# Choosing 64 tokens of 512 in eight rounds of eight largest, and a scatter with two transfers in flight in place of eight

## The reference

```python
x = x + _L0_xattn_ref(_layernorm(x), ctx, ...)   # map attention
x = x + _L0_ffn_ref(_layernorm(x), ...)          # token choice, below
x = x + _L1_xattn_ref(_layernorm(x), ctx, ...)   # attention to the context
x = x + _L1_ffn_ref(_layernorm(x), ...)          # 32 routed experts, 6 per token, and 2 shared ones
```

```python
k = max(1, int(T * CAPACITY))                         # 64 of 512 tokens in each batch
scores = jnp.einsum('btd,d->bt', hidden_states, w_router)
_, idx = jax.lax.top_k(scores, k)
idx = jnp.sort(idx, axis=-1)
sel = hidden_states[b, idx]                           # 256 rows go through attention and an MLP
...
gated = gate * processed + (1.0 - gate) * x           # gate = sigmoid of the row's score
output = hidden_states.at[b, idx].set(gated.reshape(B, k, D))
```

## Time and profile before

| | us |
|---|---|
| median of 3 runs | 2518.43 (2517.94 to 2521.67) |
| the profiled execution, its own time | 2518.06 |
| its span, first to last instruction | 2516.1 |
| token choice, first normalized tile to first gather product | 153.56 to 210.57 |
| scatters, first to last issue | 1275.93 to 1399.72 |
| TensorE busy in the whole span | 1986.4 (79%) |
| VectorE busy | 1068.8 (42%) |
| GpSimd busy | 1147.9 (46%) |
| ScalarE busy | 530.5 (21%) |

### The profile page before, as it was taken

The page is one execution under the profiler, slowest core; times in us unless marked ns, Lnnn a source line. Parts: engine busy times, 40 slices in busy tenths (PEclk is TensorE's granted clock), DMA queues, the critical chain, the costliest instruction groups (busy, mean ns, idle before and its releaser), DMA issues.

```text
span 2516.1 us, 33335 instructions
## 1 busy us (share of the span) xinstructions
PE 1986.4 (79%) x10460; PEld 1427.2 (57%) x10461; DVE 1068.8 (42%) x2094; ACT 530.5 (21%) x1132; POOL 1147.9 (46%) x578
## 2 busy tenths in 40 slices
PE   6925887968845789986762599999999999999910
PEld 3413443433312333333751599999999999999910
DVE  2573442057664667753840243333333333333300
ACT  3300221101102455441110121121122112112200
POOL 0000000003552655553357204776855878781886
PEclk8966997989975899999885799999999999999965
DMA  3052003221124444542135112555544545552999
GB/s 106 0 152 80 15 27 116 93 76 51 67 83 129 152 147 159 165 151 60 46 141 207 60 44 73 179 156 161 181 157 149 176 153 188 172 183 76 204 159 192
DMA packets 200086, 307.42 MB, mean 122 GB/s; under 512 B 16673, under 2 KB 95153, under 8 KB 199761
## 3 DMA queue, kind: packets, MB, share of 16 engines
q1 hardware_dynamic: 129744, 180.77, 22.6%
q0 software_dynamic: 21504, 50.74, 8.9%
q10 hardware_dynamic: 48768, 74.98, 8.9%
HBM read 188.33 MB, written 118.10 MB: 122 GB/s over the span
## 4 chain that ended last, share of the span: by engine, by line
PE 40%; issue 5%; POOL 5%; DMA 1%; DVE 1%; ACT 0%; SPq 0%; POOLq 0%; DVEq 0%; ACTq 0%
PE psum L2122 15%; PE psum L2142 8%; PE psum L2127 8%; POOL X L1748 5%; PE psum L2147 4%; PE psum L2109 3%; PE psum L2116 2%; DMA X<-d_y,f_slots 1%; DVE r_score L1915 1%; PE psum L2080 0%; PE psum L2072 0%; DMA r_w_gate<-in_L_ffn_gate_w 0%; DVE r_score L1916 0%; DVE e_gu_low L1886 0%; ACT r_hot L1767 0%
## 5 line engine op out<-in xcount | busy, mean ns | idle before, releaser
L2122 PE MATMUL psum<-e_gu_high,e_rowT_high 128*128 (+1 forms) x1272 | 430.1, 340 | 10.3 <-issue 10.2
L2122 PE MATMUL psum<-e_gu_low,e_rowT_high 128*128 (+1 forms) x1272 | 412.1, 326 | 4.0 <-issue 4.0
L1775 ACT ACTIVATE e_silu<-psum 128x352 f32<-128x352 f32 x159 | 74.0, 466 | 961.0 <-PE psum L2127 850.4
L2127 PE MATMUL psum<-e_gu_high,e_rowT_low 128*128 (+1 forms) x1272 | 258.7, 325 | 22.2 <-DVE e_rowT_low L1843 12.8
L2122 PEld LDWEIGHTS psum<-e_gu_high,e_rowT_high 128*128 128x128 f32 x1272 | 241.4, 190 | 31.5 <-issue 26.8
L2122 PEld LDWEIGHTS psum<-e_gu_low,e_rowT_high 128*128 128x128 f32 x1272 | 242.5, 191 | 8.6 <-issue 4.3
L1685 POOL TENSOR_TENSOR e_gu_high<-e_gu_in,e_ones 128x1408 fp32r<-128x1408 f32 x33 | 83.7, 2536 | 323.4 <-PE psum L2127 315.9
L2127 PEld LDWEIGHTS psum<-e_gu_high,e_rowT_low 128*128 128x128 f32 x1272 | 215.3, 190 | 23.2 <-DVE e_rowT_low L1843 13.1
L2142 PE MATMUL psum<-e_d_high,e_midT_high 128*128 (+3 forms) x477 | 190.4, 399 | 46.5 <-issue 45.6
L1852 DVE TENSOR_TENSOR e_midT_low<-psum,e_midT_high 128x256 fp32r<-128x256 f32 x159 | 67.5, 425 | 350.8 <-ACT e_midT_high L1784 323.0
L2142 PE MATMUL psum<-e_d_low,e_midT_high 128*128 (+3 forms) x477 | 189.4, 397 | 0.0
(11 more groups left out here) (338 smaller groups left out, 3693.6 us busy)
## 6 DMA issues: line engine op xcount, KB each, us to landing
d_sorted<-y_zeros SPq DMA_DIRECT2D x32, 1040.0 KB, 8.6
d_y<-e_y ACTq DMA_DIRECT2D x127, 256.0 KB
e_row<-d_sorted ACTq DMA_DIRECT2D x125, 260.0 KB
e_gu_in<-in_L_ffn_w_gate SPq DMA_DIRECT2D x32, 704.0 KB, 4.4
e_gu_in<-in_L_ffn_w_up SPq DMA_DIRECT2D x32, 704.0 KB, 5.1
e_d_in<-in_L_ffn_w_down SPq DMA_DIRECT2D x32, 512.0 KB, 4.4
d_y<-y_zeros SPq DMA_DIRECT2D x8, 1024.0 KB, 5.5
e_d_in<-in_L_ffn_w_down SPq DMA_DIRECT2D x32, 192.0 KB, 4.9
```

The costliest lines, as they stand in the source:

```text
L2122: nc.tensor.matmul(bank[:, 0:M].unsqueeze(1), rowT_high[par][:, k, :], w[:, bass.ds(buffer, 1), k, at:at + M], start=(k == 0 and n == 0), ...
L2127: last = nc.tensor.matmul(bank[:, 0:M].unsqueeze(1), rowT_low[par][:, k, :], gu_high[:, bass.ds(buffer, 1), k, at:at + M], start=False, st ...
```

## The change

Token choice: ScalarE writes the normalized tiles as scale times X plus `shift`, VectorE only reduces them. The scores are transposed to one row of 512 for each batch on four partitions. Eight rounds of the eight largest (`max`) and their replacement by -3e38 (`match_replace`) mark 64 tokens; a running sum over the marks gives their slots, which are transposed back. The round trip of the scores through DRAM is gone. The residual adds come behind the one-hot tiles. SP issues the heads' weights, behind the small loads and with no wait. Scatter: `SCATTERS` is 2. The diff, with its removed lines cut where the section above tells them:

```diff
             @block.sync
+                for dst, src in ((slot_base[:], c.dram["i_slot_base"]), (iota[:], c.dram["i_count"]),
...
-                sp.wait_ge(score_T_ready, 1)
-                sp.dma_start(c.dram["d_scores"], score_T[:]).then_inc(score_stored, 16)
-                sp.wait_ge(score_stored, 16)
...
+                for k in range(CC):
+                    rows = slice(k * P, (k + 1) * P)
+                    for src, at, cols in ((c.dram["L0_ffn_wq"], 0, QH * DH), (c.dram["L0_ffn_wk"], QH * DH, DH),
+                                          (c.dram["L0_ffn_wv"], (QH + 1) * DH, DH)):
+                        sp.dma_start(w_heads[:, k, :, at:at + cols],
+                                     src[rows, :].rearrange("p (h n) -> p h n", n=cols)).then_inc(heads_loaded, 16)
             @block.vector
                 norm_rows_into(nc, dve, chain, c, mv, rstd, var_ready, rstd_ready, 1e-5)
+                nc.vector.scalar_tensor_tensor(shift[:], mv[:, :, 0], -1.0, rstd[:], ALU.mult, ALU.mult).then_inc(shift_ready, 1)
                 dve.wait_ge(router_loaded, 16)
...
+                for t in range(NT):
+                    dve.wait_ge(row_ready, t + 1)
+                    last = nc.vector.scalar_tensor_tensor(unread[t], hs[:, t, :], 1.0, w_router[:], ALU.mult, ALU.mult,
+                                                          accum_out=score[:, t:t + 1])
+                last.then_inc(score_ready, 1)
+
+                dve.wait_ge(scores_turned, 1)
+                nc.vector.tensor_copy(of_batch[:], c.bank[0][0:B, :])
+                chain.link(nc.vector.tensor_copy(left[:], c.bank[0][0:B, :]))
+                for n in range(CAP // 8):
+                    chain.link(nc.vector.max(best[:, n, :], left[:]))
+                    chain.link(nc.vector.match_replace(left[:], best[:, n, :], left[:], -3e38))
+                chain.link(nc.vector.tensor_tensor(picks[:], left[:], of_batch[:], ALU.not_equal))
+                dve.wait_ge(ones_set, 1)
+                chain.link(nc.vector.tensor_tensor_scan(slot_rows[:], ones[:], picks[:], 0.0, ALU.mult, ALU.add))
+                dve.wait_ge(loaded, 5 * 16)
+                nc.vector.scalar_tensor_tensor(slot_rows[:], slot_rows[:], slot_base[:], picks[:], ALU.add, ALU.mult).then_inc(slots_found, 1)
+
+                dve.wait_ge(slots_turned, 1)
+                chain.link(nc.vector.tensor_copy(slot[:].rearrange("p (b j) -> p b j", j=JT),
+                                                 c.bank[1][:, 0:NT].rearrange("p (j b) -> p b j", b=B)))
                 nc.vector.tensor_tensor(slot_hot[:], iota[:].unsqueeze(1).broadcast_to((P, NT, P)),
                                         slot[:].unsqueeze(2).broadcast_to((P, NT, P)), ALU.is_equal).then_inc(hot_ready, 1)
+                for t in range(NT):
+                    nc.vector.tensor_tensor(c.X[:, t, :], c.X[:, t, :], hs[:, t, :], ALU.add)
                 dve.wait_ge(gathered, 1)
             @block.scalar
-                for k in range(CC):
-                    if k == CC // 2:
-
-                        act.wait_ge(scores_spread, 16)
...
+                act.wait_ge(rstd_ready, 1)
+                act.wait_ge(shift_ready, 1)
+                for t in range(NT):
+                    nc.scalar.activation(hs[:, t, :], c.X[:, t, :], ACT.Identity, bias=shift[:, t:t + 1],
+                                         scale=rstd[:, t:t + 1]).then_inc(row_ready, 1)
             @block.tensor
+                pe.wait_ge(score_ready, 1)
+                for j in range(JT):
+                    last = nc.tensor.transpose(c.bank[0][0:B, j * P:(j + 1) * P], score[:].rearrange("p (b j) -> p b j", j=JT)[:, :, j],
+                                               c.ident[:])
+                last.then_inc(scores_turned, 1)
+
+                pe.wait_ge(slots_found, 1)
+                for j in range(JT):
+                    last = nc.tensor.transpose(c.bank[1][:, j * B:(j + 1) * B], slot_rows[:, j * P:(j + 1) * P], c.ident[0:B, 0:B])
+                last.then_inc(slots_turned, 1)
...
-SCATTERS = 8
+SCATTERS = 2
```

More of the change, by code:

```diff
@@ L372, in token_choice_ffn @@
             score = sbuf(nc, stack, "b_score", [P, NT])
[L373 to L377, removed]
+            shift = sbuf(nc, stack, "b_shift", [P, NT])
+            of_batch = sbuf(nc, stack, "b_of_batch", [B, S])
+            left = sbuf(nc, stack, "b_left", [B, S])
@@ L378, in token_choice_ffn @@
+            best = sbuf(nc, stack, "b_best", [B, CAP // 8, 8])
+            picks = sbuf(nc, stack, "b_picks", [B, S])
+            ones = sbuf(nc, stack, "b_ones", [B, S])
+            slot_rows = sbuf(nc, stack, "b_slot_rows", [B, S])
             iota = sbuf(nc, stack, "b_iota", [P, P])
-            slot_base = sbuf(nc, stack, "b_slot_base", [P, NT])
+            slot_base = sbuf(nc, stack, "b_slot_base", [B, 1])
             rope = sbuf(nc, stack, "b_rope", [P, JT, DH])
-            above = sbuf(nc, stack, "b_above", [P, NT])
@@ L382, in token_choice_ffn @@
-            equal = sbuf(nc, stack, "b_equal", [P, NT])
-            chosen = sbuf(nc, stack, "b_chosen", [P, NT])
-            chosen_before = sbuf(nc, stack, "b_chosen_before", [P, NT])
             slot = sbuf(nc, stack, "b_slot", [P, NT])
             slot_hot = sbuf(nc, stack, "b_slot_hot", [P, NT, P])
-            router_loaded, loaded, var_ready, rstd_ready, score_ready, score_turned, score_T_ready, score_stored, scores_spread = sems(
-                nc, c, "b_", "router_loaded loaded var_ready rstd_ready score_ready score_turned score_T_ready score_stored scores_spread")
@@ L389, in token_choice_ffn @@
-            chosen_ready, slot_counted, hot_ready, gathered, hot_turned, chain_dve, gate_ready, gate_exp = sems(
-                nc, c, "b_", "chosen_ready slot_counted hot_ready gathered hot_turned chain_dve gate_ready gate_exp")
+            router_loaded, loaded, var_ready, rstd_ready, shift_ready, row_ready, score_ready, scores_turned, ones_set = sems(
+                nc, c, "b_", "router_loaded loaded var_ready rstd_ready shift_ready row_ready score_ready scores_turned ones_set")
+            slots_found, slots_turned, hot_ready, gathered, hot_turned, chain_dve, gate_ready, gate_exp = sems(
+                nc, c, "b_", "slots_found slots_turned hot_ready gathered hot_turned chain_dve gate_ready gate_exp")
@@ L395, in _ @@
                 sp.dma_start(w_router[:], c.dram["L0_ffn_w_router"].partition_broadcast(P)).then_inc(router_loaded, 16)
-                for dst, src in ((before[:], c.dram["i_before"]),
-                                 (tri[:], c.dram["i_tri"]), (iota[:], c.dram["i_iota"]), (slot_base[:], c.dram["i_slot_base"]),
+                for dst, src in ((slot_base[:], c.dram["i_slot_base"]), (iota[:], c.dram["i_count"]),
                                  (rope[:], c.dram["i_rope"].rearrange("(j p) d -> p j d", p=P)),
@@ L418, in _ @@
                 norm_rows_into(nc, dve, chain, c, mv, rstd, var_ready, rstd_ready, 1e-5)
+                nc.vector.scalar_tensor_tensor(shift[:], mv[:, :, 0], -1.0, rstd[:], ALU.mult, ALU.mult).then_inc(shift_ready, 1)
                 dve.wait_ge(router_loaded, 16)
[L420 to L473, removed]
+                unread = [bank[:] for bank in c.bank]
+                unread += [held[:, 4 * q:4 * q + 4, :].rearrange("p t s -> p (t s)") for held in (slot_hot, slot_hot_T) for q in range(4)]
@@ L508, in _ @@
             def _(pe):
[L509 to L513, removed]
-                nc.tensor.matmul(c.bank[1][:, 0:NT], ones[:], chosen_before[:], start=False, stop=True).then_inc(slot_counted, 1)
+                pe.wait_ge(score_ready, 1)
[7 more added lines that the diff above has]
+                last.then_inc(slots_turned, 1)
                 pe.wait_ge(hot_ready, 1)
@@ L2253, in shape_tables @@
         "i_tri": (p[:, None] < p[None, :]).astype(f),
-        "i_before": np.stack([s[None, :] < (j * P + p)[:, None] for j in range(JT)], 1).astype(f),
         "i_iota": np.broadcast_to(p.astype(f), (P, P)).copy(),
-        "i_slot_base": np.broadcast_to(((np.arange(NT) // JT % 2) * (S // 8) + 1).astype(f), (P, NT)).copy(),
+        "i_count": np.broadcast_to((p + 1).astype(f), (P, P)).copy(),
+        "i_slot_base": (np.arange(B) % 2 * (S // 8)).astype(f)[:, None].copy(),
         "i_rope": np.concatenate([np.cos(ang), np.sin(ang)], 1).astype(f),
```

5 lines of the change are left out of this document (1 added, 4 removed).

## The result

The changed kernel takes **2407.88 us** (median, 2405.06 to 2410.97) against 2520.05 for the kernel before: a ratio of 0.9552 (95%: 0.9531 to 0.9573). The forecast was 2389. Its profiled execution took 2406.69 us, 111.4 less than that of before. In the routed stage its lines are those of before less 31. Times are medians; three runs of the kernel before further down (2557.80, 3495.14 and 4688.90 us) were in a slow state and are left out of every ratio.

The account below looks back on a forecast made before the run. Bounds: a hole in the routed stage, where TensorE crawls while GpSimd scatters, and a serial token choice. 2518.1 - 24 (choice) - 108.8 (hole) + 4 (late first tile) = 2389 us; range 2380 to 2420.

Parts of the forecast that it names:

- the likeliest case: Routed stage: the hole goes, together with the token choice gain; 2389 us, own range 2380 to 2420, chance 0.50.
- the late first tile: Start of sorted tiles: about 4 us lost for a slow first part and late tile; slower scatters covered by 5 us.
- the hole: Routed stage, 1290 to 1403 us: TensorE busy only 21.97 of 113 us while GpSimd scatters; 108.8 us to come back.
- The scores and the choice: Token choice stage: scores gain 7.3 us and choice 17.5, together 24.8 us, of which 24 used.
- The moved adds and the weights: Token choice: residual adds beside gather products, and weight transfers issued by SP, cost nothing; uncovered adds would cost 9.7 us.
- The reading behind it: Routed stage: the crawl follows some eight scatters issued without looking back; pacing to landings ends it, returning 108.8 us.
- every 1.7 us: Scatters, upper end of the range: last lands at 1440, holding the first sorted tile by some 20 us; 2420 us.
- if the first routed tile waits for its row: Sign of being wrong, at the first sorted tile: forecast loaded by 1420, needed at 1426.
- The rival of 4.1 us per scatter: Scatters: landing as late as a gather becomes the pace, last lands at 1673; 2636 us, chance 0.07.
- The starved refill: Routed stage: instruction refill as tempting cause; by the queue rule the cap would give nothing, 2508 us; hole stays, 0.25.

Follow-up runs that it names:

- closed set: A set of runs on one chip in which the unchanged kernel before took 2408 to 2412 us, without the hole.
- the choice alone: Changed kernel with eight scatters in flight instead of two: 2385.13 us (ratio 0.9912) in set 1, 2495.73 us (0.9901) in set 3.
- set 1: Follow-up runs beside an unchanged kernel before at 2407.98 us: scatter caps of two, four and eight, and a 384-column pause.
- set 3: Follow-up runs on the chip of set 1, unchanged kernel before 2520.48 us: eight in flight unpaced 2495.73 us, with a 384-column pause 2399.30 us.
- set 4: Follow-up runs on a second chip, unchanged kernel before 2522.33 us: cap of four 2497.80 us, eight with a 256-column pause 2390.60 us.
- four in flight: Changed kernel with SCATTERS = 4 instead of 2: 2384.48 us (ratio 0.9908) in set 1, 2497.80 us (0.9905) in set 4.
- the short pause: Changed kernel with eight scatters in flight and a 256-column scratch clear behind each: 2390.60 us, ratio 0.9481, in set 4.
- open set: A set of runs on one chip in which the unchanged kernel before took 2520 to 2522 us, with the hole.

## Why the prediction was right, and where it was not

The time came within 19 us, inside the likeliest case's own range of 2380 to 2420. 18 of the 19 us are one term, the late first tile. That the result was measured where the hole is open was luck: in a closed set the largest term, 108.8 us, would have been nothing. By its steps:

- **The scores and the choice: 24.8 us, 24 used.** The stage gave 25.0 up to the first product. Run against run, the choice alone gives 22.9 us in set 1 and 24.8 in set 3. The rounds took 179.63 - 167.69 = 11.9 us for 12.1 forecast, the scan 1.21 for 1.2; the last reduction ended near 165.3 rather than 164.8, since ScalarE writes a tile every 0.71 us and VectorE follows it. Costing an unseen operation by its neighbours' rows at another width was right.
- **The moved adds and the weights: nothing.** Right; the adds end at 195.1 and the products at 208. The weights are issued from 151.2 to 173.1, land at most 9.6 us after that, and are first read at 219.5.
- **The hole: 108.8 us back.** Right in size: within set 4, from four in flight to the short pause, it is 2497.80 - 2390.60 = 107.2 us, which with the 4.1 us of short pieces is the whole. **The reading behind it failed.** "The crawl sets in only after some eight scatters that were issued without looking back", and "pacing to landings ends it": with eight in flight and no wait on a landing a pause of 0.33 us ends it (set 4), so pacing to landings isn't needed. Nor does it take eight without looking back: with four in flight the crawl begins as early and is whole. The cap of two slowed the scatters to 1.72 us on average, more than the 1.52 and 1.62 us that end the hole with eight in flight, so its pace is enough to account for what it did; a cap of two at the old pace can't be run, so nothing more is shown. The prediction named this beside it (1.84 us leaves TensorE alone, 1.30 does not) and drew the wrong one of the two.
- **A late first tile: 4 us, "covered by 5 us".** This is the mis-sized term. The pace was 1.72 us, not 1.45, and the row came 21.9 us late. Without stragglers a pair takes 3.0 us (1.27 and 1.73), one landing of 2.7 and 0.30 to start the next, so 1.50; what is left, 95 x 0.22 = 21 us, are single landings that come late, as the 3.60 us wait in the rows above, and the column copies. With eight allowed such a landing delays nobody; with two it stops the stream. The range had this case ("every 1.7 us ... holds the first sorted tile by some 20 us") and I did not take it as the likeliest. It is also one of the prediction's own signs of being wrong, "if the first routed tile waits for its row": that sign came, at a fifth of the hole's size.
- **The rival of 4.1 us per scatter** did not come: 2.7 us to land.
- **The rival that no case covered.** I took the hole for a property of the kernel. It is one of kernel and set together, since the choice alone took 2385.13 us in set 1 and 2495.73 in set 3, on one chip. In a closed set the change as a whole was not run; worked out from set 1, it is 2407.98 + 24.4 - 22.9 = 2409.5 us, so no change: the cap gives back what the choice gains.
- **The starved refill.** By the Trainium skill, "DMA: Bandwidth & Descriptors", Queues, rings and completion order, a DMA engine takes turns between its queues packet by packet; no run here shows the turns themselves. That a refill was not what TensorE waited for is borne out by set 3, where its single steps and the wait of 43.59 us ended with no instruction packet on record. So the rule led the right way on the cause. But the time that I had worked out with it, 2508 us, took a cap to change nothing, and the cap changes the pace.

**What stays open** is what opens the hole in one set and not in another, and which resource GpSimd's issues and TensorE share. No experiment here varied either: the sets differ in nothing that I chose, other than the kernels run in them. Whether it is the scatters' pace as such, their bytes or rows per time, or the gap in which GpSimd issues none, was not parted either. The cap alone (old choice stage) was not run in an open set. All the runs had the profiler's record of the granted clock. The Trainium skill, "NOTIFIC — the notification-queue block", 7.1 Overflow: three behaviours, one of which stalls the engine, says that this block's inner pipeline holds its producers back rather than lose a record, so the recording itself could be the queue that fills; no run here shows it or excludes it.

The best version for open sets is the choice with eight in flight and the pause of 256 columns: 2390.6 us, faster than both kernels. In a closed set it was not run; its neighbours with 128 and 384 columns took 2384.1 and 2398.8 there, both faster than the kernel before beside them, by 1.2% and 0.4%.

## What to carry to other kernels

If an engine crawls while the engine beside it issues indirect transfers back to back, try a short pause between issues before a cap on those in flight: here a cap of two tied the stream to its late landings (2406 us), and a pause didn't (2391). And before an unnamed release is put down to the nearest product, follow the kernel to the one that it needs. Before a gain of many per cent is put down to an edit, run both kernels in more than one set, and see what the kernel before does in each. A cover of 5 us under a stream of 96 steps is no cover when the pace is uncertain by 0.2 us.

## What the runs showed of the hardware that I had not expected

- One and the same kernel had two times 4.6% apart (2385.13 us in set 1 and 2495.73 in set 3 for the choice alone), alike within a set, on one chip. By the kernel before it was the slower one in the three open sets and in the runs that the prediction was made from.
- In an open set single matmuls stood up to 3.5 us apart, and ScalarE was released 80 us after the end of the product that it needed (set 3). The DMA engines had a share of 0.53 there, and 0.53 too under the short pause, where TensorE was full (set 4).
- In open sets 1.27 us from issue to issue, with pauses at the column copies, has the whole hole, and 1.46 us leaves 4 us of it. Nothing between was run in an open set.
- MAX8 and MATCH_REPLACE8 take 0.68 and 0.67 us over 512 columns, as an ordinary operation of that width; the scan takes 1.21.
